# Narrow cross attentions: projection, bias and turning handed over bank by bank, turning ahead of the tally, queries spread three steps ahead

## The reference

```
q_len, S2, DCA, H, HD = 64, 112, 16, 16, 16      # the context's 128 tokens: 112 main, 16 "dca"
x = layernorm(x)
q     = _ln((x @ Wq + bq).reshape(b, s1, H, HD), qn_w, qn_b)       # layer norm over each head's 16
k     = _ln(y_main @ Wk + bk), kn_w, kn_b) ;  v     = y_main @ Wv + bv
k_dca = _ln(y_dca @ Wkv_dca[:, :256] ...)  ;  v_dca = y_dca @ Wkv_dca[:, 256:] ...
ctx   = softmax(q k^T / 4) v + softmax(q k_dca^T / 4) v_dca
out   = x + ctx @ Wo + bo
```

## Time and profile before

| | |
|---|---|
| median of three runs | 3049.25 us |
| the profiled execution | 3051.77 us, span 3050.0 us |
| TensorE busy in the span | 2726.3 us (89%) |
| VectorE, ScalarE, GpSimd busy | 1881.7, 1395.4, 1042.4 us |
| mean granted clock of TensorE | 0.968 |
| one narrow cross attention, first score to last project_out (L1) | 881.3 to 1061.9 us of the span |

### The profile page before, as it was taken

How to read it: one execution, slowest core, us unless ns; L and a number is a source line. 1 busy time by engine, 2 the same in 40 slices (tenths; PEclk the granted TensorE clock), 3 DMA queues, 4 the chain that set the end, 5 groups by cost and what they waited for, 6 DMA issues and landing times. The chain is left out here.

```text
span 3050.0 us, 51289 instructions
## 1 busy us (share of the span) xinstructions
PE 2726.3 (89%) x19376; PEld 1712.3 (56%) x19376; DVE 1881.7 (62%) x2536; ACT 1395.4 (46%) x2672; POOL 1042.4 (34%) x884
## 2 busy tenths in 40 slices
PE   7999987999989898899989877679988899899899
PEld 5999953466556647433346533236643555554687
DVE  3666646222258737434468689867855999996342
ACT  3233344122257647322256654646767656653123
POOL 1222300133135524000036400015611899991562
PEclk9999999999999999999999988899999999999999
DMA  4000005111210000200000000000011121113224
GB/s 159 21 28 21 17 7 176 62 47 45 69 33 2 9 16 2 86 1 0 9 14 2 16 0 0 1 23 2 2 42 38 59 81 69 71 47 114 63 88 148
DMA packets 77017, 128.94 MB, mean 42 GB/s; under 512 B 12112, under 2 KB 54737, under 8 KB 76305
## 3 DMA queue, kind: packets, MB, share of 16 engines
q1 hardware_dynamic: 67888, 101.78, 10.1%
q0 software_dynamic: 8928, 24.39, 2.6%
HBM read 107.40 MB, written 18.74 MB: 41 GB/s over the span
## 5 line engine op out<-in xcount | busy, mean ns | idle before, releaser
L3502 POOL TENSOR_TENSOR h<-ssm_u,ss_bc 128x1024 f32<-128x1024 f32 x88 | 205.8, 2360 | 0.1
L3465 ACT ACTIVATE ssm_p_h<-ss_delta,ss_decay 128x256 f32<-128x256 f32 x352 | 146.6, 464 | 126.8 <-DVE ctxT L3539 85.3
L3412 PE MATMUL ssm_p_y<-ctxT,ident 128*128 128x512 f32 x412 | 188.8, 598 | 0.0
L684 POOL TENSOR_TENSOR xw_prob<-xw_prob,xw_rsum 128x512 f32<-128x512 f32 x64 | 65.3, 1041 | 257.5 <-DVE xw_rsum L633 257.5
L3534 DVE TENSOR_TENSOR_SCAN ssm_p_h<-ssm_p_h,h 128x1024 f32<-128x1024 f32 x64 | 145.8, 2279 | 8.9 <-ACT ssm_p_h L3465 6.8
L3492 POOL TENSOR_TENSOR ctxT<-ctxT,ss_bc 128x1024 f32<-128x1024 f32 x50 | 117.6, 2359 | 21.8 <-DVE ctxT L3532 21.8
L3412 PEld LDWEIGHTS ssm_p_y<-ctxT,ident 128*128 128x128 f32 x412 | 77.2, 194 | 80.3 <-issue 79.4
L3396 PE MATMUL ssm_p_h<-ssm_b_diagonal,ssm_uT 128*128 128x128 f32 x640 | 86.2, 292 | 39.9 <-DVE ctxT L3539 20.6
L515 PE MATMUL xw_p_q<-h,xw_m_h 128*128 (+1 forms) x1024 | 118.6, 277 | 1.3 <-PEq L60 1.3
L515 PEld LDWEIGHTS xw_p_q<-h,xw_m_h 128*128 128x128 f32 x1024 | 115.5, 192 | 6.7 <-issue 6.7
L523 PE MATMUL xw_p_q<-xw_u,xw_vo_h 128*128 128x128 f32 x1024 | 117.1, 275 | 1.2 <-ACT xw_u L587 1.2
(11 more groups left out here) (878 smaller groups left out, 7198.8 us busy)
## 6 DMA issues: line engine op xcount, KB each, us to landing
ss_bc<-ss_bc_rows SPq DMA_DIRECT2D x24, 896.0 KB, 4.3
xw_ctx_rows<-in_ctx_rows SPq DMA_DIRECT2D x32, 256.0 KB, 2.6
ss_bc<-ss_bc_rows SPq DMA_DIRECT2D x8, 768.0 KB, 4.1
L3f_rows<-L3f_rows_out SPq DMA_DIRECT2D x16, 384.0 KB, 4.2
L0f_wg<-in_L_ffn_gate SPq DMA_DIRECT2D x9, 512.0 KB, 9.8
L0f_wu<-in_L_ffn_up SPq DMA_DIRECT2D x9, 512.0 KB, 9.7
L0f_wd<-in_L_ffn_down SPq DMA_DIRECT2D x9, 512.0 KB, 9.7
L0f_rows<-L0f_rows_out SPq DMA_DIRECT2D x16, 256.0 KB, 4.0
```

The costliest lines, as they stand in the source:

```text
L684: g.tensor_tensor(prob[:, n % 2, part, :], prob[:, n % 2, part, :], bcast(rsum[:, 1, part], 2, S2), ALU.mult).then_inc(sem["normed"], 1)
L3412: mm = pe.matmul(p_y[:, 2 * half:2 * half + 2, :].rearrange("p e t -> p (e t)"), k.ident[:, :], weighed[n % RING_W][:, ts(half, CH)], star ...
L3465: i = act.activation(out[:, ts(e, CT)], delta[:, e, ts(c, CT)], ACT.Exp, scale=decay[:, E4 * s + e:E4 * s + e + 1])
L3502: g.tensor_tensor(tiles(drive[n % RING]), u[:, c % 2, :, :], bcast(bcs[:, row_b(s), :], 1, E4), ALU.mult).then_inc(sem["driven_g"], 1)
```

## The change

It makes four edits, all in `cross_attention_narrow`.

1. `projected` and `biased` are raised once for each bank, so `add_bias` takes a bank as soon as it is projected, and `turn` takes a bank as soon as it is biased. A projection waits bank by bank too for the reading of the turned probabilities.
2. On TensorE, `turn` stands ahead of `tally`.
3. On ScalarE, `squares` stands ahead of the copies of the turned probabilities, and `inverse` behind them.
4. On GpSimd, the queries are spread three batches ahead, at the beginning of a step, where they were spread two ahead at its end.

```diff
@@ tensor
-            def turned_before(n):
+            def turned_before(n, half=1):
                 if n >= 3:
-                    pe.wait_ge(sem["turned_read"], 2 * (n - 2))
+                    pe.wait_ge(sem["turned_read"], 2 * (n - 3) + half + 1)
                 else:
                     pe.wait_ge(ln.sem["normed"], NCH)
-            def project(i):
+            def project(i, n=None):
...
                 for o in range(H2):
+                    if n is not None:
+                        turned_before(n, o)
...
-                    if i == 1 and o == 0:
-                        mm.then_inc(sem["projected_half"], 1)
-                mm.then_inc(sem["projected"], 1)
+                    mm.then_inc(sem["projected"], 1)
             def widen(i):
...
-                pe.wait_ge(sem["biased"], i + 1)
+                pe.wait_ge(sem["biased"], 2 * i + 2)
-            def turn(n):
+            def turn(n, units):
...
                 for o in range(H2):
+                    for i, part in units:
+                        if part == 0:
+                            pe.wait_ge(sem["biased"], 2 * i + o + 1)
+                        elif part == 2:
+                            pe.wait_ge(sem["scaled"], i + 1)
                     if n >= 1:
                         pe.wait_ge(sem["turned_read"], 2 * n + o - 1)
@@ tensor, step
                     if part == 0:
-                        turned_before(n)
-                        project(i)
+                        project(i, n)
...
                 if within(n, 3, B + 3):
                     mix(n - 3)
+                if within(n, 2, B + 2):
+                    turn(n - 2, units + at_step(n - 1) if n == 2 else units)
                 for i, part in units:
                     if part == 1:
...
                         tally(i)
-                if within(n, 2, B + 2):
-                    for i, part in units:
-                        if part == 0:
-                            pe.wait_ge(sem["biased"], i + 1)
-                        elif part == 2:
-                            pe.wait_ge(sem["scaled"], i + 1)
-                    turn(n - 2)
@@ scalar
             def add_bias(i):
-                act.wait_ge(sem["projected"], i + 1)
                 if i >= 2:
                     act.wait_ge(sem["scaled"], i - 1)
                 for o in range(H2):
-                    j = from_product(i, biased[:, i % 2, :, :], o, ACT.Identity)
-                j.then_inc(sem["biased"], 1)
+                    act.wait_ge(sem["projected"], 2 * i + o + 1)
+                    from_product(i, biased[:, i % 2, :, :], o, ACT.Identity).then_inc(sem["biased"], 1)
             def biased_squares(i):
...
                 for o in range(H2):
-                    if i == 1 and o == 0:
-                        act.wait_ge(sem["projected_half"], 1)
-                    else:
-                        act.wait_ge(sem["projected"], i + 1)
+                    act.wait_ge(sem["projected"], 2 * i + o + 1)
@@ scalar, step: behind the copy of the mix
                 for i, part in units:
-                    if part == 1:
-                        inverse(i)
+                    if part == 0:
+                        squares(i)
                 if within(n, 2, B + 2):
...
                 for i, part in units:
-                    if part == 0:
-                        squares(i)
+                    if part == 1:
+                        inverse(i)
@@ vector, add_bias (unit 0 alone)
-                v.wait_ge(sem["projected"], i + 1)
                 v.wait_ge(sem["copied"], 2)
                 for o in range(H2):
+                    v.wait_ge(sem["projected"], 2 * i + o + 1)
...
-                j.then_inc(sem["biased"], 1)
+                    j.then_inc(sem["biased"], 1)
@@ gpsimd
             def step(n):
+                if n + 3 < B:
+                    spread_q(n + 3)
                 if within(n, 1, B + 1):
...
                     if part == 2:
                         affine(i)
-                if n + 2 < B:
-                    spread_q(n + 2)
...
             spread_q(1)
             affine(2)
+            spread_q(2)
```

More of the change, by code:

```diff
@@ L1389, in cross_attention_narrow @@
         k.prefix = f"{layer}x_"
-        sem = semaphores(nc, ctx, k.prefix, "projected_half merged_keys merged merged_bias merged_out copied projected biased squared tallied logged inverse widened scaled ready out_bias "
+        sem = semaphores(nc, ctx, k.prefix, "merged_keys merged merged_bias merged_out copied projected biased squared tallied logged inverse widened scaled ready out_bias "
                                             "zeroed valued v_main v_copied q_spread scored maxed shifted exped summed recip normed "
@@ L1695, in add_bias @@
                 for o in range(H2):
-                    j = from_product(i, biased[:, i % 2, :, :], o, ACT.Identity)
-                j.then_inc(sem["biased"], 1)
+                    act.wait_ge(sem["projected"], 2 * i + o + 1)
+                    from_product(i, biased[:, i % 2, :, :], o, ACT.Identity).then_inc(sem["biased"], 1)
             def squares(i):
-                act.wait_ge(sem["biased"], i + 1)
+                act.wait_ge(sem["biased"], 2 * i + 2)
                 if i >= 2:
```

## The result

The changed kernel takes 3015.14 us, the median of four runs (3012.98 to 3018.03), against 3049.27 for the kernel before, timed beside it: a ratio of 0.9885 with a 95% interval of 0.987 to 0.990. The forecast was 3026 with a range of 3019 to 3041.

A forecast was written before the change was run, and what follows sets the result against it. The prediction took TensorE as the bound, busy 101.42 of 107 us in L1's middle stretch, VectorE next. Gains of 25.1 us less 2.1 taken back by VectorE left 23, giving 3026; 8-in-10 range 3019 to 3041.

The forecast's parts named there:

- ahead of the steps: Before the first score, bias and squares by bank start earlier on ScalarE: 0.7 us a stage, 2.1 in three stages.
- first tally and unit 4's start (steps 1 to 3): At the first tally, earlier bias and turn inside the tally's wait save 1.3 us a stage, 3.9 in three.
- odd tallies with the step behind: Steps 5, 11, 17, 23: turn ahead of tally shortens mix to widening by 0.25 us, 3.0 in 12 steps.
- even tallies: Steps 8, 14, 20: the turn covers the tally's wait, gaining 0.8 us each, 7.4 in 9 steps.
- projecting steps: The turn's five waits for the bias, 0.8 us a stage, vanish: 2.4 in three stages.
- queries three ahead: At n = 26 the score no longer waits for spread queries: 1.11 us a stage, 3.3 in three.
- clock in step 26: TensorE's clock drop after the wait for spread queries goes away: 1.49 us each, 3.0 for two stages.
- taken back by VectorE: In the twenty-one tally steps, VectorE takes back a fifth of the 10.4 us gain, 2.1.
- The increments: Some 33 more semaphore increments on TensorE, taken at zero cost; 0.03 us each, 1.0 in all, as the other end.
- VectorE as the bound step for step: Rival: VectorE takes back the tally and bias terms (12.8 us) in the steps, giving 3037; chance 0.16.
- Idle time that only moves: Rival: ScalarE's queue loses what moved instructions gain; only 5.4 us from prologue and spread remain, 3044; chance 0.08.
- The mix waiting for turned copies: Rival: squares ahead delay turned copies and the next mix in 24 projecting steps, 13.4 us slower, 3063; chance 0.04.

The follow-up runs named there:

- vector_dose: The changed kernel with a fill on VectorE in steps 4 to 24, longer from L1 to L2 to L3; 3019.65 us, ratio 0.9888.
- banks_only: The kernel before with only the first edit, projected and biased raised by bank; 3033.18 us, ratio 0.9943.
- turn_only: The kernel before with only the second and third edit, turn ahead of tally and ScalarE's new order; 3033.06 us, ratio 0.9938.
- before_shifted: The kernel before with six more warm matmuls at the beginning of L1's stage; 3058.19 us, ratio 1.0015.
- after_again: The changed kernel unaltered, run again on another chip; 3027.17 us, ratio 0.9895 to the kernel before, which took 3057.82 there.
- squares_behind: The changed kernel with ScalarE's squares put back behind the copies of the turned probabilities; 3015.61 us, ratio 0.9888.
- after: The changed kernel itself, with all four edits on the kernel before; 3015.14 us, ratio 0.9885.

## Why the prediction was right or wrong

Terms over three stages, in us:

| term | forecast | measured |
|---|---|---|
| ahead of the steps | 2.1 | 2.4 |
| first tally and unit 4's start (steps 1 to 3) | 3.9 | 6.7 |
| odd tallies with the step behind | 3.0 | 2.8 |
| even tallies | 7.4 | 7.8 |
| projecting steps | 2.4 | 3.8 |
| queries three ahead | 3.3 | 3.8 |
| clock in step 26 | 3.0 | 3.0 |
| taken back by VectorE | -2.1 | 0 |
| outside of the stages | 0 | 3.8 |
| sum, median to median | 23.0 | 34.1 |

The 11.1 us between the two sums are 3.8 outside of the stages, 2.8 at the first tally, 2.1 of VectorE, 1.4 in the projecting steps and 1.0 in all the rest.

**Right:** which waits would go, in which steps, what is late behind each, and that the edits pay one by one. Odd and even tallies came to 0.24 and 0.87 a step, forecast 0.25 and 0.8. In the even step the widening follows the mix's end by 3.3 us (992.66 to 995.94), as forecast.

**The step that failed** is "I let it take back a fifth of the gain of the twenty-one tally steps (10.4), 2.1". It rested on a share, 83%, and not on a row in which TensorE waited for VectorE. This is the whole list of TensorE's waits in L1's middle stretch after the change (903 to 1001 us); VectorE is not in it:

```profile
PE L1x_p_t L1563 <- issue: 1.2, 3, 0.5
```

`vector_dose` shows the room behind that: 0.38 us in all steps but one. That VectorE works off its backlog from a short tally step in the long projecting ones is my reading; no run isolates it. The only thing VectorE took back is the 0.4 of step 27, and that was in the forecast's 1.11. This step is a fifth of what was missed; the rest is terms of the right kind and the wrong size, and what lies outside of the stages.

**Mis-sized: the first tally**, "Three stages: 3.9". The chain itself, 1.75 less in step 2 and 0.19 more in step 3, makes 1.56 a stage, 4.7; I had taken 1.3. The bias by banks gave 0.74 of it in `banks_only`, forecast 0.78. The part behind gave 0.83, forecast 0.6: from the tally to the widening it was 1.88 (899.29 to 901.17 in L1) in place of 2.71, where I had put the two turned copies and the inverse one behind the other for 2.1. The first copy had begun at 899.14, ahead of the tally. The other 2.0 lie where the clock differed: in `turn_only` alone step 1 takes 7.00 us in L1 (granted clock 0.76) and 8.93 in L2 and 8.94 in L3 (0.52), though the stages are alike; in L1 step 3 then took 6.59 in place of 5.07, at 0.74. "The start of unit 4's projection itself does not gain more" held (12.77 us behind the first score before, 12.68 after), but the price of a projection at the low level (4.10 against 2.16) had no term of its own. It varies with no change at all: in the unaltered kernel before, it took 3.75, 3.82 and 4.08 in the three stages.

**Mis-sized: projecting steps**, 2.4 against 3.8. I multiplied printed idle time. Printed, the turn waited 0.16; by starts, the step got 0.23 shorter. A group's busy time reaches past the start of the next group when they are back to back: the mix is printed as 0.65, but the turn starts 0.59 behind it. So each printed wait is 0.06 to 0.08 short. The tally's 0.27 was 0.35 in the same way. In step 4 the weaker wait ahead of the projection, taken at nothing, gave another 0.12.

**Outside of the stages**, taken at 0, is the largest part of the miss, and it does not repeat. The stages alone reach 3018.9 from the median before, just under the range of 8 in 10 (from 3019) and the forecast's own end (3020). The other 3.8 us lie outside of them. The span less the three stages was 2465.5 us in the profiled execution before, and 2462.4 in `before_shifted` without its added matmuls; with the change it was 2457.9, 2472.8 in `after_again`, and 2458.7 to 2465.7 in `squares_behind` and the three with the bias on ScalarE. So the rest of the kernel moves by up to 15 us for the same program, and these traces show no gain in it from the change. What repeats is the gain of the stages: they sum to 584.4 and 583.1 us in the two traces of the kernel before, and to 554.1, 554.7 and 554.0 in `after`, `after_again` and `squares_behind`, 28 to 30 us less. The 3.8 on top are not shown to be the change's.

**The increments.** Steps that project queries have one more increment in the middle of their matmuls, and took 6.75 and 7.65 us in `banks_only` against 6.76 and 7.65. So it costs nothing that 0.02 us could hide. The Trainium skill ("TensorE: Matmul & The Clock Gate", The cost: per-tile semaphore tail) fits 26.3 ns for each increment in the tail behind matmuls on concurrent tiles; the matmuls here run one behind the other, and by these steps they pay no such price.

**The rivals.** VectorE as the bound step for step (3037): refuted by the doses. Idle time that only moves (3044): refuted by the three single edits. The mix waiting for turned copies (3063): the list has one such wait, 0.3 at the end of the stage, and had the same before; and `squares_behind` is 0.1 us a stage slower, not faster.

## What to carry to other kernels

Where stages run in fixed steps, compare starts of the same instruction from step to step: it repeats to 0.02 us here, while the times of whole executions of one kernel spread over 5 to 14 us, and it prices an edit of 0.1 us. Keep steps with a low clock out of such sums. Deduct for another engine only where a row shows a wait for it, or dose it with fills until something appears. In an in-order queue, put behind each other what waits for the same thing last: the turn needed nothing that the tally waited for.

## What the runs showed that I had not expected

The wait for spread queries was followed by a low clock in 8 of the 12 stages of the four traces that have it (step 26 at 5.73 to 5.78, granted clock 0.70), and in the other four not (4.21 to 4.22, at 1.00). In the 24 stages of the eight traces without the wait it never came: 4.21 or 4.22 in each. I had put the other end of this term at 0; the return is as reliable as the wait's removal, while the drop before is a matter of luck. So the term depends on the execution before: with no drop in it the clock would give nothing back, and with one in each stage an estimated 4.5 us (1.5 for each, from the two stages that had it).
